# The first unit's rows of maxima brought onto the operands' partitions by TensorE, and a later count for the third chunk of the setup

## What is computed

```python
xn = _layernorm(x)
qkv = xn @ w_attn + b_attn                       # q, k, v: 16 heads of 8 columns
scores = einsum('bhqd,bhkd->bhqk', q, k) * 8 ** -0.5
scores += mask        # -log(k - q + 1) where k > q, 0 where k == q, -inf where k < q
out = einsum('bhqk,bhkd->bhqd', softmax(scores), v) @ w_proj + b_proj
ffn = fp4_linear(silu(fp4_linear(xn, w_gate)) * fp4_linear(xn, w_up), w_down)
return x + out + ffn
```

## Time and profile before

| | us |
|---|---|
| median of 3 runs | 604.85 |
| lowest and highest | 604.67, 604.93 |
| the profiled execution, its own time | 605.48 |
| its span | 603.8 |
| busy in it: PE, DVE, POOL, ACT | 557.4, 548.3, 541.9, 398.9 |
| granted clock of TensorE, mean over the span | 0.995 of full speed |

### The profile page before, as it was taken

The page is one execution under the profiler, slowest core; times in us unless marked ns, Lnnn a source line. Parts: engine busy times, 40 slices in busy tenths (PEclk is TensorE's granted clock), DMA queues, the critical chain, the costliest instruction groups (busy, mean ns, idle before and its releaser), DMA issues.

```text
span 603.8 us, 11270 instructions
## 1 busy us (share of the span) xinstructions
PE 557.4 (92%) x3791; PEld 249.6 (41%) x3791; DVE 548.3 (91%) x1165; ACT 398.9 (66%) x868; POOL 541.9 (90%) x409
## 2 busy tenths in 40 slices
PE   5999999999898989898989999998999898999985
PEld 3668754444343434234333433343344243343323
DVE  5999989998999999999998999999898989999662
ACT  4677476675665667665767576667656767677792
POOL 7277999898999999899999999998999899899883
PEclk9999999999999999999999999999999999999998
DMA  6344344010000001000000000000000000000000
GB/s 194 95 116 108 109 103 107 2 67 14 2 3 1 2 1 68 30 1 2 1 1 1 19 1 2 1 2 2 1 2 18 2 0 2 2 1 1 2 2 17
DMA packets 14832, 16.66 MB, mean 28 GB/s; under 512 B 1639, under 2 KB 14216, under 8 KB 14360
## 3 DMA queue, kind: packets, MB, share of 16 engines
q1 hardware_dynamic: 14240, 15.70, 9.4%
q10 hardware_dynamic: 536, 0.26, 0.2%
HBM read 11.75 MB, written 4.01 MB: 26 GB/s over the span
## 4 chain that ended last, share of the span: by engine, by line
POOL 49%; PE 34%; ACT 8%; issue 3%; DMA 3%; SPq 1%; DVE 0%; POOLq 0%; ACTq 0%
POOL ring L895 41%; PE psum L1467 9%; PE psum L1425 8%; PE psum L1449 6%; ACT ring L1049 3%; PE psum L1310 2%; DMA kop<-parts_dram 2%; POOL xw L913 2%; POOL xw L911 2%; POOL xw L915 2%; PE psum L1381 1%; ACT kop L931 1%; PE psum L1452 1%; PE psum L1400 1%; PE psum L1428 1%
## 5 line engine op out<-in xcount | busy, mean ns | idle before, releaser
L895 POOL TENSOR_TENSOR ring<-ring,dist 128x1024 f32<-128x1024 f32 (+3 forms) x223 | 438.8, 1999 | 22.6 <-ACT ring L1049 22.4
L1240 DVE TENSOR_REDUCE mxp<-psum 128x1 f32<-128x512 f32 (+3 forms) x640 | 356.6, 604 | 19.2 <-PE psum L1425 16.1
L1049 ACT ACTIVATE ring<-psum 128x512 f32<-128x512 f32 (+3 forms) x446 | 211.2, 530 | 99.2 <-PE psum L1452 47.0
L1425 PE MATMUL psum<-kop,qop 96*128 96x512 bf16 (+3 forms) x640 | 197.1, 351 | 5.6 <-DVE mxp L1240 2.7
L1449 PE MATMUL psum<-qop,kop 128*128 128x512 bf16 (+3 forms) x640 | 189.6, 349 | 4.4 <-DVE mxp L1240 1.3
L1467 PE MATMUL psum<-ring,vaug 128*32 128x512 f32 (+3 forms) x1280 | 149.9, 540 | 15.5 <-POOL ring L895 13.3
L1267 DVE TENSOR_TENSOR ring<-psum,dist 128x512 f32<-128x512 f32 (+3 forms) x194 | 115.9, 625 | 12.4 <-ACT psum L1049 11.8
L1049 ACT ACTIVATE psum<-psum 128x512 f32<-128x512 f32 (+3 forms) x194 | 99.5, 545 | 36.7 <-PE psum L1449 22.4
L1425 PEld LDWEIGHTS psum<-kop,qop 96*128 96x128 bf16 x640 | 56.4, 97 | 125.6 <-DVE mxp L1240 41.3
L1449 PEld LDWEIGHTS psum<-qop,kop 128*128 128x128 bf16 x640 | 59.3, 97 | 73.1 <-DVE mxp L1240 13.1
L1428 PE MATMUL psum<-tri_q,identb 128*128 128x128 bf16 x256 | 56.0, 221 | 0.0
(11 more groups left out here) (134 smaller groups left out, 483.3 us busy)
## 6 DMA issues: line engine op xcount, KB each, us to landing
parts_dram<-qpart SPq DMA_DIRECT2D x18, 128.0 KB, 3.3
kop<-parts_dram SPq DMA_DIRECT2D x6, 384.0 KB
qop<-parts_dram SPq DMA_DIRECT2D x6, 384.0 KB
xin<-_attn_hidden_states_dram SPq DMA_DIRECT2D x4, 256.0 KB, 4.8
ring<-inv_dram SPq DMA_DIRECT2D x1, 1024.0 KB, 5.1
out_dram<-xin SPq DMA_DIRECT2D x4, 256.0 KB, 2.3
qop<-parts_dram SPq DMA_DIRECT2D x3, 288.0 KB
kop<-parts_dram SPq DMA_DIRECT2D x3, 288.0 KB
```

The lines of the kernel that those rows point to most:

```text
L895: g_.tensor_tensor(slot(p)[:, :, 0:n], slot(p)[:, :, 0:n], both, ALU.mult).then_inc(weighed_pool, 1)
L1049: a_.activation(scores if pair_vec[p] else slot(p)[:, e % 2, 0:n], scores, ACT.Exp, scale=SCALE).then_inc(exp_done, 1)
L1240: v_.tensor_reduce(mxp[:, u % 2, 4 * a + j, c - g:c - g + 1], bank(*o)[:, 0:n], AX_X, ALU.max).then_inc(max_used, 1)
L1425: ins = mm(bank(*o)[:, 0:n], qop[0:K_MAX, u // NQ % 2, h, P * a:P * (a + 1)], kop[0:K_MAX, h, k0:k0 + n], start=True, stop=(c != g))
```

## The change

Unit 0 gets a path of its own. `parts` and `minor` write its three parts into a new tile `lifted`, 96 columns further on, head by head. For each half of the unit (two of its four heads) a new item `lift` has TensorE transpose 99 columns of `lifted` eight times, so that the three parts land on partitions 96 to 98 of a PSUM bank, and ScalarE copies these three partitions, 1024 elements each, straight to `qop`. The item `rows` of unit 0 with its transposes, its copy and its three DMAs is gone, and so is the wait for those DMAs: the first product of unit 0's second pass waits for the copy. The rank of `minor` of unit 0 becomes -1, ahead of everything else on GpSimd. The other units keep the path that they had, and unit 3 no longer waits for unit 0's transfer, since unit 0 has no `mrow`. The counts at which semaphores are awaited are moved to match. GpSimd clears `lifted` once in the setup. The third chunk of the setup may be taken at a count of 30 blocks instead of 2; the fourth keeps its 60.

```diff
-CHUNK_AT = [0, 0, 2, 60]
+CHUNK_AT = [0, 0, 30, 60]
...
             needs = [("DVE", item)] + ([("POOL", ("minor", u - 2))] if k == 0 and u >= 2 else
-                                       [("PE", ("rows", u - 2))] if k and u >= 2 else [])
+                                       [("PE", ("rows", u - 2) if u > 2 else ("lift", 1))] if k and u >= 2 else [])
             vec(("parts", u, k), 64, needs, rank=0)
-        pool(("minor", u), 740, [("DVE", ("parts", u, 1))], rank=0)
+        pool(("minor", u), 740, [("DVE", ("parts", u, 1))], rank=0 if u else -1)
+        if u == 0:
+            for half in range(2):
+                pe(("lift", half), 8 * P, [("POOL", ("minor", 0))], rank=0)
+                act(("lift", half), 2 * GQ, [("PE", ("lift", half))], rank=0)
+            continue
...
-        needs = [("DMA", ("rows", u))]
+        needs = [("DMA", ("rows", u)) if u else ("ACT", ("lift", e % 4 // 2))]
...
+        lifted = sb("lifted", [P, MROW + TPG * 4 * PARTS], BF16)
...
+        def part_of(u, i):
+
+            if u == 0:
+                return lifted[:, MROW:].rearrange("p (a j i) -> p a j i", a=TPG, j=4)[:, :, :, i]
+            return mpart[:, u % 2, :, i]
...
+            g_.memset(lifted[:], 0.0).then_inc(pool_seq, 1)
...
-                    if u >= MROWS:
-                        act.wait_ge(mrow_loaded[u % MROWS], 16 * PARTS * (u // MROWS))
+                    if u > MROWS:
+                        act.wait_ge(mrow_loaded[u % MROWS], rows_loaded(u - MROWS))
...
+                if o[0] == "lift":
+                    act.wait_ge(mT_psum, o[1] + 1)
+                    a_.activation(qop[MROW:MROW + PARTS, 0, 2 * o[1]:2 * o[1] + 2, :].rearrange("p h n -> p (h n)"),
+                                  bank(*o)[MROW:MROW + PARTS, 0:GQ].bitcast(BF16), ACT.Identity).then_inc(mT_ready, 1)
...
+                if o[0] == "lift":
+                    bank_free(*o)
+                    pe.wait_ge(mparts_ready, 1)
+                    rows = bank(*o)[0:MROW + PARTS, 0:GQ].bitcast(BF16)
+                    for j in range(2):
+                        for a in range(TPG):
+                            c0 = PARTS * (4 * a + 2 * o[1] + j)
+                            ins = nc.tensor.transpose(rows[:, GQ * j + P * a:GQ * j + P * (a + 1)],
+                                                      lifted[:, c0:c0 + MROW + PARTS], identb[:])
+                    ins.then_inc(mT_psum, 1)
...
                     if b == NT - 1 and e % 4 == 0:
-                        pe.wait_ge(mrow_loaded[u % MROWS], 16 * PARTS * (u // MROWS + 1))
+                        if u:
+                            pe.wait_ge(mrow_loaded[u % MROWS], rows_loaded(u))
+                    if u == 0 and b == NT - 1 and e % 2 == 0:
+                        pe.wait_ge(mT_ready, e % 4 // 2 + 1)
```

28 lines of the change are left out of this document (16 added, 12 removed).

## The result

The changed kernel takes 612.88 us (median; 610.68 to 613.56), the kernel before 604.76 in the same comparison (603.13 to 604.93): a ratio of 1.0134, 95% interval 1.0103 to 1.0165. The forecast was 604.1 with a range of 599 to 609. It failed on the side of slower, by 8.8 us, and 3.9 us beyond the range.

The account below looks back on a forecast made before the run. No engine alone was taken to set the time, with TensorE, VectorE and GpSimd all near full. Terms +1.5 - 12 + 9.7 = -0.8 us on a span of 603.8 turned the median of 604.85 into 604.1 us, range 599 to 609.

Parts of the forecast that it names:

- minor first: Unit 0 on GpSimd: minor goes ahead of the split at 37.60, starting 2.2 us earlier.
- lift: Unit 0: sixteen transposes take about 1.1 us, two 3-partition ScalarE copies 2.1 us, delaying second-chunk transfers some 2 us, costed 0.
- first head: Start of the second pass: first head near 41.5 instead of 50.03, 8.5 us sooner.
- the gate: First pv, needing all 200 fills and freeing slots for heads beyond the sixteenth: opens 1.5 us later, at 78.1.
- The 8.5 us: The first head's earlier start at unit 0, forecast to be gone at the first pv because the eight slots fill earlier.
- the forecast's own signs of being wrong: First pv before 74, VectorE gaps before it, or units 13 to 15 taking other than 120 to 127 us.
- the third chunk at no cost: Setup's third chunk at count 30: transfers not needed until unit 8, past 167 us; cost 0.
- To unit 12: Run up to unit 12's parts: all three queues grow, by 2.0, 2.0 and 1.1; taken +1.5, bounds 0 and +2.5.
- the queue sums: Each engine's listed items added at their spacing; VectorE's whole queue 540.7 before and 543.3 after.
- Units 13 to 15: From unit 12's parts to unit 15's: 1.041 times the longest queue, 117.2, gives 122.0; taken -12 us.
- The tail: Behind the last maximum: 84 heads instead of 69, 24 pv instead of 19; taken +9.7 us, bounds 7.9 and 11.
- The longer tail is not paid for: Rival: units 13 to 15 save only 8.1, tail costs 9.7 to 11; +3.6 to +4.9, so 609; chance 0.22.

Follow-up runs that it names:

- b_lift: Kernel before, its lists kept, with unit 0's rows item replaced in place by the two lift items on TensorE and ScalarE; 605.08 us, 1.0030.
- a_fill100: Changed kernel with 100 fills instead of 200; 612.07 us, 1.0129 against the kernel before.
- b_chunk30: Kernel before with only the third chunk's count at 30 instead of 2; 614.10 us, 1.0167.
- b_left88: Kernel before with the maxima run further ahead from unit 14 on, leaving 88 heads behind the last maximum instead of 69; 606.26 us, 1.0048.
- a_table: Changed kernel plus a one-column exponential behind the setup's last square root, so the table load moves there; 611.64 us, 1.0119 against the kernel before.
- a_fill205: Changed kernel with 205 fills instead of 200, its lists falling back into those of before at head 218; 606.76 us, 1.0042 against the kernel before.
- b_fill204: Kernel before with 204 fills instead of 200; 608.15 us, 1.0086.
- b_pairs: Kernel before with the changed kernel's choice of engine for each pair (101 pairs on VectorE), the rest planned anew; 608.73 us, 1.0089.

## Why the prediction was wrong, by its own steps

**Right in its times: minor first, lift, first head.** `minor` started at 37.85 (foretold 37.60), sixteen transposes took 1.07 us (1.1), a copy of 3 partitions and 1024 elements 0.97 us (1.0), the first head stood at 41.58 (41.5). The choice of the upper bound for the copy was right: its cost goes by the length of the row. The `p2` copy came at 42.41 instead of 39.92, 2.5 us later (2), and nothing waited for its transfers. Wrong was the reason for the 8.06 us from the first DMA issue to the first head: TensorE had no gap ahead of that head at 50.03, its list put products for maxima and fills there, and in b_lift the head stays late without the transfers. That had no part in the sum.

**Right in kind: the gate.** The sixteen heads fill the slots and the second pass stands still (ScalarE 1.91 of 10 us at 70 to 80). The 8.5 us were lost there as foretold, and opening the gate earlier (a_fill100) did not bring them back.

**Wrong in two steps: the time of the gate.** The first `pv` came at 81.86, not 78.1. I had taken VectorE's queue and let 3.0 us more of TensorE disappear "mostly into its own waits". From unit 0's maxima to the first `pv`, before and after:

```profile
36.36:76.60 40.24, 39.76 (x347) 31.90 (x345) 39.86 (x102) 24.12 (x52) 33.66 (x40) 1.00 0.40 111
```

```profile
36.62:81.86 45.24, 42.73 (x377) 34.05 (x375) 43.43 (x104) 25.55 (x53) 35.22 (x41) 1.00 0.40 104
```

TensorE had no waits to take them: with the fills in its list it was busy for 39.76 of 40.24 us. Its 3.0 us more show in full, and it waits 2.0 us more besides (2.5 and 0.5), the longest 1.09 us at its fourth head, for a bank that ScalarE had not read yet behind the table load, and 0.35 at 80.90, for GpSimd's `xw` of the rounding. VectorE, which was to have no gap, has 1.8 us of idle time there (before 0.4); that is one of the forecast's own signs of being wrong. The error of 3.8 us did not reach the end: unit 4 was earlier than before.

**Right: the third chunk at no cost in this kernel.** No stall at it here. But b_chunk30 shows that this is a matter of the list: with the same count and another order around it, it cost one wait of 5.22 us.

**Failed: "To unit 12 ... I take +1.5".** It was +5.2. VectorE's busy time between the maxima of unit 0 and those of unit 12 grew by 2.6 us (371.1 to 373.7), which the queue sums had as 2.0; its idle time grew by 2.4 (14.9 to 17.3), which they cannot have. I took less than the growth of the queue where more was to be taken. The other 0.3 us lie ahead of unit 0's maxima.

**Failed: "Units 13 to 15 ... I take -12".** It was -9.8, at the lower part of the bounds of -8.1 to -14. The factor of 1.041 on the longest queue does not carry over from one list to another: here 125.0 us stand against 117.2 of VectorE's queue, 1.067. 1.4 of the 2.2 us missed may be the one wait at 434.75 with TensorE at half speed, a term that the sum did not have.

**Failed: "The tail ... I take 9.7".** It was +12.3, over both bounds. VectorE's busy time there grew by 9.2 and its idle time by 3.1; 0.9 of it is TensorE's clock in the last steps. The sum had put the growth of VectorE's idle time at next to nothing, since `silu` was to fit in its gaps.

The three misses add up, 3.7 + 2.2 + 2.6 = 8.5 us, since all have one sign. What was wrong in all three is the same thought: that the idle time of one list carries over to another, or shrinks. My terms had an outcome of -0.8 for a kernel whose VectorE queue I had myself summed to 2.6 us more (540.7 and 543.3). They thus foretold that VectorE would idle 3.4 us less than before, and nothing in the profile spoke for that; from unit 0 on it idled 4.1 more. With the queue sum alone and before's idle time the forecast would have been 607.5, inside the range and on the right side.

**The rivals.** "The longer tail is not paid for" had its condition met: the units 13 to 15 gave 9.8 us, under the 10 from which it decides, and the direction was its own. But its terms account for 2.5 of the 7.7 us, and b_left88 shows that with another list the same tail is nearly paid for. No rival had what holds the most: that VectorE idles more over the whole of a list planned anew, also where the change touches nothing.

**How much chance is in a list.** Nine of the kernels run (after among them, and a_table, which has after's lists, not counted) have a list of their own that is new over most of the run. From unit 0 on they need 4.2 to 9.2 us more than before, whatever made them new: lift, rank, count, fills, a fixed division. VectorE idles 47.2 to 54.2 us in them, against 46.6. Two that are new only behind head 412 or 484 need 0.6 and 0.8 more. Three in which before's list stands again from head 218 on, or throughout, lie between -1.7 and +1.3. Before's list is at the good end of these, and any entry that moves all of it had much to lose and little to win. That the new list carries most of the loss is shown by a_fill205 (0.4% with all of the change, and before's list behind head 218) together with b_fill204 and b_pairs (0.9% with nothing of the change). Why before's is good, and which of its placements a new list would have to keep, the runs do not settle. What they show is where the price is seen. The view of VectorE's waits (engine, tile and line, releaser: us in total, times, longest), from unit 10 to unit 12 and behind the last maximum, before:

```profile
DVE mxp L1240 <- PE psum L1425: 1.6, 3, 0.9
...
DVE ring L1267 <- ACT psum L1049: 11.0, 11, 4.8
```

and after:

```profile
DVE mxp L1263 <- PE psum L1448: 3.5, 6, 1.3
...
DVE ring L1290 <- ACT psum L1068: 12.4, 15, 2.2
```

In these two stretches it is many short waits, for products of the maxima and in the tail for exponentials, not one long one. That fits it that no single undone step brought the time back.

## What to carry to other kernels

Where one greedy plan makes a fixed order for several engines, a change of any entry must be priced in two parts: what it does by itself, and what the new order around it costs; the second was up to 9 us here and the first 1 to 2.5. Test an edit inside the old order first (put in by hand, or with a knob that makes the plan fall back into it), and test an unrelated entry beside it, to see how far the lists scatter. When the terms of a sum imply that the fullest engine will idle less than before, name what removes that idle time, or take its growth in work as the least that is to be expected.
